# Graph network kernel: norm, query/key/value products and walk table merged into one stage

## What is computed

```python
# layer 0: relational sum, residual and norm
xt  = einsum('ni,rio->rno', x, W0)                 # 8 relations
agg = segment_sum(xt[edge_type, dst], src)         # rows by relation and node
x1  = layernorm(x + relu(agg + bias))
# layer 1: attention over the edges, 8 heads of 32
Q, K, V = x1 @ Wq, x1 @ Wk, x1 @ Wv
score = (K[src] * Q[dst]).sum(head) / sqrt(32) + edge_weight
attn  = softmax of score over the edges of one dst
out   = segment_sum(attn * V[src], dst) @ Wp + bp
# then two layer norms around a GELU network of width 1024,
# the residual x1 and a last layernorm
```

## Time and profile before

| | us |
|---|---|
| median of 3 runs | 5518.05 (5516.32 to 5522.2) |
| the profiled execution, its own time | 5525.3 |
| its span | 5523.6 |
| mid and walk stages in it, from 2551.2 to 2829.0 | 277.8 |

### The profile page before, as it was taken

The page is one execution under the profiler, slowest core; times in us unless marked ns, Lnnn a source line. Parts: engine busy times, 40 slices in busy tenths (PEclk is TensorE's granted clock), DMA queues, the critical chain, the costliest instruction groups (busy, mean ns, idle before and its releaser), DMA issues.

```text
span 5523.6 us, 88413 instructions
## 1 busy us (share of the span) xinstructions
PE 4353.1 (79%) x19107; PEld 2903.1 (53%) x19107; DVE 4710.7 (85%) x15317; ACT 3282.0 (59%) x8872; POOL 3212.9 (58%) x3363
## 2 busy tenths in 40 slices
PE   7998777777777767554848888888888888887997
PEld 3444444344444444443536666666666666665556
DVE  6888999999999998555269999999999999995555
ACT  2888777777777777000236666666666666662222
POOL 2003777777777777772047777777777777760000
PEclk9999999999999999776979999999999999998999
DMA  5433333333333333335347777777777777762000
GB/s 171 132 126 113 105 105 104 105 104 105 105 105 103 101 104 105 105 105 112 118 142 214 215 215 212 212 212 209 212 212 209 212 212 209 211 187 65 6 16 24
DMA packets 349148, 778.95 MB, mean 141 GB/s; under 512 B 76928, under 2 KB 179927, under 8 KB 348629
## 3 DMA queue, kind: packets, MB, share of 16 engines
q0 software_dynamic: 214080, 658.04, 41.8%
q1 hardware_dynamic: 129138, 111.40, 6.4%
q10 hardware_dynamic: 5410, 3.83, 0.2%
HBM read 691.39 MB, written 81.59 MB: 140 GB/s over the span
## 4 chain that ended last, share of the span: by engine, by line
PE 27%; DVE 14%; issue 9%; DVEq 2%; POOL 1%; ACT 1%; DMA 0%; POOLq 0%; ACTq 0%; SPq 0%
PE pb L1412 11%; DVE node_a L1558 4%; PE pb L1396 4%; PE pb L1782 3%; PE pb L1791 3%; DVE big L1516 2%; PE pb L1123 2%; DVE big L1544 1%; DVEq L325 1%; PE pb L1803 1%; PE pb L1129 1%; DVE peak L1583 1%; DVE peak L1585 1%; DVE top L1565 1%; PE pb L1447 1%
## 5 line engine op out<-in xcount | busy, mean ns | idle before, releaser
L1376 POOL DMA_INDIRECT big<-kv_table,walk_s x1664 | 1586.1, 953 | 575.0 <-issue 478.1
L694 POOL DMA_INDIRECT big<-xt_table,big x1616 | 1554.8, 962 | 535.7 <-issue 496.8
L703 ACT ACTIVATE walk_s<-walk_s,big 128x128 bf16<-128x128 bf16 x4704 | 1499.3, 390 | 426.7 <-DVE walk_s L968 402.5
L841 PE MATMUL pb<-big,walk_s 128*128 128x256 f32 x3232 | 1035.1, 417 | 243.8 <-issue 128.5
L1412 PE MATMUL pb<-big,early 128*128 128x264 f32 x3328 | 841.2, 396 | 105.0 <-issue 84.8
L1008 DVE TENSOR_TENSOR node_a<-node_a,pb 128x256 f32 x1616 | 662.9, 410 | 258.1 <-PE pb L841 248.5
L1396 PE MATMUL pb<-node_a,hot_t 128*128 x3328 | 819.7, 389 | 28.8 <-issue 22.8
L841 PEld LDWEIGHTS pb<-big,walk_s 128*128 128x128 f32 x3232 | 621.3, 208 | 385.9 <-DVE walk_s L1032 155.7
L768 PE MATMUL pb<-walk_s 128*128 128x384 bf16 x1568 | 531.5, 339 | 349.6 <-ACT walk_s L703 317.7
L1412 PEld LDWEIGHTS pb<-big,early 128*128 128x128 f32 x3328 | 601.6, 191 | 227.2 <-issue 118.0
L1396 PEld LDWEIGHTS pb<-node_a,hot_t 128*128 128x128 f32 x3328 | 602.9, 191 | 112.9 <-issue 47.2
(11 more groups left out here) (275 smaller groups left out, 5573.3 us busy)
## 6 DMA issues: line engine op xcount, KB each, us to landing
xt_table<-big SPq DMA_DIRECT2D x98, 512.0 KB, 2.9
big<-kv_table,walk_s POOLq DMA_INDIRECT x1664, 3.7
big<-xt_table,big POOLq DMA_INDIRECT x1616
pens<-pen_table SPq DMA_DIRECT2D x832, 12.1 KB
kv_table<-big SPq DMA_DIRECT2D x49, 256.0 KB, 2.0
x_store<-big SPq DMA_DIRECT2D x49, 128.0 KB, 2.0
big<-in_x POOLq DMA_DIRECT2D x48, 128.0 KB, 3.3
big<-in_x SPq DMA_DIRECT2D x6, 1024.0 KB, 11.4
```

The lines of the kernel that those rows point to most:

```text
L694: e.indirect_dma_start(sum_rows[:, q % SUM_ROWS, k, :], None, xt_table, bass.IndirectOffsetOnAxis(ap=idx_all[:, i:i + 1], axis=0))\
L703: ins = e.activation(hot_v[:, t % SORT_HOTS, v, :], hot_q[:, t % SORT_HOTS, :], ACT.Copy, scale=byte[:, t:t + 1])
L841: e.matmul(pb[:, SUM_AT + i % SUM_BANKS, 0:D], sum_hot[:, i % SUM_HOTS, :], sum_rows[:, q % SUM_ROWS, k, :], start=True, stop=True).then_i ...
L1376: e.indirect_dma_start(rows[:, q % ROW_RING, k, 0:2 * D], None, kv_table, bass.IndirectOffsetOnAxis(ap=src_i[:, i:i + 1], axis=0))\
```

## The change

The mid and the walk phase become one. SP, ACT, DVE, TensorE and POOL each run both parts in one order. The buffers of `x` and the walk's records no longer share a region: `x1` becomes a ring of 35 tiles plus one slot for the last tile. The `x` loads are eight (x_loads), Wq, Wk and Wv stand behind the first of them, and loads 5 and 6 (tiles 35 to 42 and 43 to 47) wait until tiles 0 to 7 and 0 to 12 have been stored and transposed. The moments are turned into scales in chunks of eight tiles on DVE alone, by an integer first guess and four Newton steps (`inverse_root`), in place of the one square root on ACT and the reciprocal. Tile w is normalised in step w+10 of DVE's loop and its query copied in step w+13. The walk's DVE instructions are the same and stand in fixed steps of the loop. The query has two PSUM banks in place of four, and banks 6 and 7 serve the walk's matmuls. The ends and carries go through POOL's queue in place of SP's. `dst_i` is `dl_f` now, and `u_row` lies in `hot_t`. The edge phase and everything after it are unchanged.

```diff
+        X_RING = 35
+        x1m = cut((X_RING + 1) * D).rearrange("p (w d) -> p w d", d=D)
+        root_w = cut(2 * 8)
+        def inverse_root(e, c, y, x, t):
+            c(e.tensor_scalar(t.bitcast(I32), x.bitcast(I32), 1, None, ALU.arith_shift_right))
+            c(e.tensor_scalar(y.bitcast(I32), t.bitcast(I32), -1.0, float(0x5f3759df), ALU.mult, ALU.add))
+            for _ in range(4):
+                c(e.tensor_tensor(t, y, y, ALU.mult))
+                c(e.scalar_tensor_tensor(t, t, -0.5, x, ALU.mult, ALU.mult))
+                c(e.scalar_tensor_tensor(y, t, 1.5, y, ALU.add, ALU.mult))
...
+        x_loads = [(0, 8), (8, 16), (16, 24), (24, 32), (32, X_RING), (X_RING, 43), (43, W - 1), (W - 1, W)]
+        NORM_LAG = CHUNK + 2
+        Q_LAG = NORM_LAG + 3
+        REC_AT = 25
...
         def mid_io(e):
+            load(0)
             for n, name in enumerate(("L1_gnn_Wq", "L1_gnn_Wk", "L1_gnn_Wv")):
...
+            load(1)
             e.wait_ge(s_upad, 1)
...
+            for k in (2, 3, 4):
+                load(k)
+            e.wait_ge(s_xpad, 1)
+            load(7)
+            for w in range(W):
+                e.wait_ge(s_norm, w + 1)
+                e.dma_start(x1_store[w * P:(w + 1) * P, :], xs_of(w)).then_inc(s_x1st, 16)
+                e.wait_ge(s_kvc, w + 1)
+                e.dma_start(kv_table[w * P:(w + 1) * P, :], kv_out[:, w % 2, :]).then_inc(s_kvst[w % 2], 16)
+                for k in (5, 6):
+                    if w == x_loads[k][1] - X_RING - 1:
+                        e.wait_ge(s_x1st, 16 * (w + 1))
+                        e.wait_ge(s_nt, w + 1)
+                        load(k)
...
+            def root(ws):
+                lo, n = ws[0], len(ws)
+                c.upto(c.n)
+                c(e.tensor_scalar(root_w[:, 0:n], moments[:, lo:lo + n, 1], EPS, None, ALU.add))
+                inverse_root(e, c, rstd[:, lo:lo + n], root_w[:, 0:n], root_w[:, CHUNK:CHUNK + n])
+                c(e.scalar_tensor_tensor(nmr[:, lo:lo + n], moments[:, lo:lo + n, 0], -1.0, rstd[:, lo:lo + n],
+                                         ALU.mult, ALU.mult))
...
+            for m in range(W + Q_LAG):
+                if m < W:
+                    relu_add(m)
+                if 0 <= m - 1 < W:
+                    count(m - 1)
+                if 0 <= m - 2 < W:
+                    moment(m - 2)
+                    if (m - 2) % CHUNK == CHUNK - 1 or m - 2 == W - 1:
+                        root(chunks[(m - 2) // CHUNK])
+                w = m - NORM_LAG
+                if 0 <= w < W:
+                    if w == 0:
+                        c(e.memset(acc_w[:, :, D:AW], 0.0))
+                    e.tensor_scalar(xs_of(w), xs_of(w), rstd[:, w:w + 1], nmr[:, w:w + 1], ALU.mult, ALU.add)\
+                        .then_inc(s_norm, 1)
+                w = m - Q_LAG
+                if 0 <= w < W:
+                    e.wait_ge(s_qkv, 2 * w + 2)
+                    e.tensor_copy(acc_w[:, w + 1, 0:D], pb[:, 4 + w % 2, 0:D]).then_inc(s_qc, 1)
+                if m == 11:
+                    walk_ends()
+                if m == 15:
+                    walk_spread()
+                if 16 <= m < 16 + WALK_G:
+                    walk_tiles(m - 16)
+                if m == 16 + WALK_G:
+                    walk_index()
+                    select_consts()
+                if 33 <= m < 37:
+                    walk_row(m - 33)
+                if m == 37:
+                    walk_table()
+                if m == 38:
+                    pens_ends()
+                if 39 <= m < 45:
+                    k, odd = divmod(m - 39, 2)
+                    if odd:
+                        pens_out(k)
+                    else:
+                        pens_flag(k)
+                if m == 50:
+                    carries_out()
+                if m == 53:
+                    locals_of()
...
         def mid_tensor(e):
...
+                if w >= 2:
+                    e.wait_ge(s_qc, w - 1)
...
+                if w == 1:
+                    e.wait_ge(s_ucol, 1)
+                    spread(u_col, 0, 4, 6)
+                    spread(u_col, 4, UG, 7).then_inc(s_urow, 1)
+                b = w - 19
+                if 0 <= b < 4:
+                    if b == 0:
+                        e.wait_ge(s_tcol, 1)
+                    if b >= 2:
+                        e.wait_ge(s_wrowd, b - 1)
+                    spread(t_col, 4 * b, min(4 * b + 4, WALK_G), 6 + b % 2).then_inc(s_trow, 1)
+                if 0 <= w - REC_AT < WALK_G:
+                    turn_records(w - REC_AT)
...
         def mid_scalar(e):
-            e.wait_ge(s_stat, 1)
-            e.activation(rstd[:], rstd[:], ACT.Sqrt).then_inc(s_sq, 1)
...
+                if 0 <= w - 1 - REC_AT < WALK_G:
+                    keep_records(w - 1 - REC_AT)
...
-        phase(sync=walk_io, gpsimd=walk_gather, vector=walk_vector, tensor=walk_tensor, scalar=walk_scalar)
+        phase(sync=mid_io, gpsimd=mid_gather, vector=mid_vector, tensor=mid_tensor, scalar=mid_scalar)
```

More of the change, by code:

```diff
@@ L1076, in mid_vector @@
[L1076 to L1131, removed]
@@ L1253, in walk_vector, with locals_of, bias_mask, bias_add @@
+            def locals_of():
+                e.wait_ge(s_recc, 3 * WALK_G)
+                c(e.scalar_tensor_tensor(dl_f, w_row, -float(P), dl_f, ALU.mult, ALU.add))
+            def bias_mask(bound, op):
                 c(e.tensor_scalar(w_tmp, dl_f, bound, LOW, op, ALU.mult))
+            def bias_add():
                 c(e.tensor_tensor(wgt_i, wgt_i, w_tmp, ALU.add))
[L1256 to L1258 removed]
@@ L1266, in walk_vector @@
-            e.sem_inc(s_pens, 1)
-            e.wait_ge(s_endin, 32)
-            first, last = ends_in[0:CHUNKS, :, 0], ends_in[0:CHUNKS, :, 1]
-            con, who = cont[0:CHUNKS, :], whole[0:CHUNKS, :]
-            base, step = (carry_out[0:CHUNKS, k * 2 * SPAN:(k + 1) * 2 * SPAN].rearrange("p (s c) -> p s c", s=2)
-                          for k in range(2))
-            c(e.memset(carry_out, LOW))
-            c(e.memset(step[:, 0, 0:1], 0.0))
-            c(e.memset(cont, 0.0))
-            c(e.tensor_tensor(con[:, 1:SPAN], first[:, 1:SPAN], last[:, 0:CH], ALU.is_equal))
@@ L1283, in walk_vector @@
-            c(e.tensor_scalar(step[:, 1, 1:CH], step[:, 1, 1:CH], 1.0, -LOW, ALU.subtract, ALU.mult))
-            e.sem_inc(s_carry, 1)
-        def walk_tensor(e):
-            def spread(col, n):
-                for g in range(n):
-                    ins = e.matmul(pb[:, g // 4, (g % 4) * P:(g % 4 + 1) * P], col[:, g:g + 1].to_broadcast([P, P]),
+            e.memset(xs_of(W - 1), 0.0).then_inc(s_xpad, 1)
+            e.memset(u_col, 1e6).then_inc(s_upad, 1)
+            for m in range(W + Q_LAG):
[36 more added lines that the diff above has]
+                        pens_out(k)
+                    else:
+                        pens_flag(k)
[3 more added lines that the diff above has]
+                    locals_of()
+                if m == 54:
+                    c(e.tensor_copy(dl_b, dl_f))
+                if m == 55:
+                    bias_mask(0.0, ALU.is_lt)
+                if m == 56:
+                    bias_add()
+                if m == 57:
+                    bias_mask(float(P), ALU.is_ge)
+                if m == 58:
+                    bias_add()
@@ new lines, in mid_tensor, with turn, spread @@
+        def mid_tensor(e):
+            def turn(w):
+                e.wait_ge(s_norm, w + 1)
+                if w >= 2:
+                    e.wait_ge(s_ntc, w - 1)
+                for k in range(KC):
+                    ins = e.transpose(pb[:, w % 2, k * P:(k + 1) * P], xs_of(w)[:, k * P:(k + 1) * P], ident[:])
+                ins.then_inc(s_nt, 1)
+            def spread(col, lo, hi, bank):
+                for g in range(lo, hi):
+                    ins = e.matmul(pb[:, bank, (g - lo) * P:(g - lo + 1) * P], col[:, g:g + 1].to_broadcast([P, P]),
@@ L1310, in walk_scalar @@
                         .then_inc(s_recc, 1)
-        phase(sync=walk_io, gpsimd=walk_gather, vector=walk_vector, tensor=walk_tensor, scalar=walk_scalar)
+            turned(0)
+            for w in range(W):
+                if w + 1 < W:
+                    turned(w + 1)
+                e.wait_ge(s_qkv, 2 * w + 1)
+                if w >= 2:
+                    e.wait_ge(s_kvst[w % 2], 16 * (w // 2))
+                e.activation(kv_out[:, w % 2, :], pb[:, 2 + w % 2, :], ACT.Copy).then_inc(s_kvc, 1)
+                if 0 <= w - 1 - REC_AT < WALK_G:
+                    keep_records(w - 1 - REC_AT)
```

303 lines of the change are left out of this document (172 added, 131 removed).

## The result

| us | before | changed kernel |
|---|---|---|
| median of 4 runs | 5520.12 (5516.32 to 5522.82) | 5419.65 (5417.96 to 5428.29) |
| ratio | | 0.9822, 95% interval 0.9805 to 0.9839 |
| profiled execution, its span | 5525.3, 5523.6 | 5420.85, 5419.1 |
| start of the stage, start of the edge stage | 2551.2, 2829.0 | 2543.0, 2719.4 |
| length between the two | 277.8 | 176.4 |

The time fell by 100.5 us, where the prediction had 100.9; 5419.65 stands against a forecast of 5417. The stage that changed is 101.4 us shorter. The rest of the two profiles also differs, by 8.2 us before the stage and 5.1 us after it in the other direction, though no instruction there was changed; the experiments come back to that.

What follows compares the result with a forecast made beforehand. TensorE was taken to bound the merged stage: first transpose 2569.6 + 149.6 work + 7 stalls = 2726.2, edge stage 1.9 later at 2728.1 instead of 2829.0. That is 100.9 us off the 5518.05 median: 5417 us, range 5405 to 5434.

Steps and rivals of the forecast that it cites:

- front, start of the stage to first transpose: Start of the merged stage: scales after ten tile sums let TensorE's first transpose come at 2569.6, 27.0 us earlier.
- a root: DVE, seven times, once per chunk: a chain of 16 small instructions at 0.21 us, 3.4 us each.
- load 1 late: Second x load, behind Wq, Wk and Wv: lands near 2562.8, wanted at 2563.1; cost 0, at worst 4 us.
- TensorE's work: First transpose to last product: 140.7 us plus 8.9 for added spreads and transposes, 149.6 us.
- waits for norms: TensorE stalls where DVE's norms come late in the merged loop: 7 us in all, bounds 0 and 20.
- records, gathers, stores, query banks late: Queues and waits beside TensorE's work: records have 4.4 us of slack; cost taken as 0, at most 4 us.
- The queue of DVE: DVE's loop: lateness up to 4.2 us is free, each step repays 1.4 us, the rest stalls TensorE, 7 us.
- upper bound of 20 us: Worst TensorE stalls: all walk and root work of steps 16 to 30 and 39 to 45 beyond 1.4 a step.
- Gathers held by DVE: Rival: each of 13 POOL gathers waits for one DVE instruction, 1 to 11 us lost, 5418 to 5428; chance 0.07.
- DVE becomes the bound: Rival: root instructions of 0.47 us or more make roots 7.5 us, 15 to 25 us lost, 5432 to 5442; chance 0.08.
- TensorE loses its clock: Rival: stalls in the merged stage drop the granted clock to 0.50, work becomes 299 us, 5560; chance 0.01.
- The edge stage: Stage after the merged one: may find TensorE's clock up, worth at most 2 to 3 us, taken as 0.

Runs made afterwards that it cites:

- run without walk pieces: Changed kernel with the walk's pieces taken out of the tile loops into a phase of their own behind the products: 5483.68 us, 0.9935 of the kernel before.
- spread run: Changed kernel with the same walk pieces in other steps of DVE's loop, long ones kept apart from roots: 5411.68 us, 0.9805 of the kernel before.
- run with one block moved: Kernel before, with only the block of local targets and bias moved behind the penalties and carries: 5509.15 us, 0.9980 of the kernel before.

## Why the prediction was right

| step of the prediction | predicted | changed kernel |
|---|---|---|
| front, start of the stage to first transpose | 18.4 | 17.9 |
| a root | 3.4 | 3.2 |
| load 1 late | 0 | 0.2 at most |
| TensorE's work | 149.6 | 150.7 busy (149.7 and 149.5 in the other two profiles) |
| waits for norms | 7 | 5.9 |
| records, gathers, stores, query banks late | 0 | 0 |
| last product to edge stage | 1.9 | 1.9 |
| stage | 176.9 | 176.4 |

- **What bounds it.** The reading of the earlier trace rows, that TensorE's middle stretch stays and everything beside it can hide, is what carried the number; no term missed by over 1.1 us. The misses also cancel in part (front 0.5 short, work 1.1 long, waits 1.1 short), and the changed kernel's medians lie between 5415.3 and 5419.7 us, so that the agreement to 0.4 us is luck and that to some 5 us is not.
- **The roots.** Taking 0.21 us from the chain of 128x13 instructions in place of 0.33 from 128x256 was right (0.20).
- **The queue of DVE.** The prediction let backlog up to 4.2 us cost nothing, let each step repay 1.4 us, and placed the losses at the roots of steps 17 and 25 and in steps 39 to 44. The waits stand there: 0.54 against 0.4, 1.32 against 1.9, and at the flags four with 3.7 in all against five with 4.9. The run without walk pieces and the spread run (no wait after the second tile in either) show that it is large pieces too close together, and not the roots or the walk's work as such. The upper bound of 20 us for these waits does not come out of the pieces that it names, which give some 12 to 17 by its own prices; the forecast's own worse bound, 85 us less, would have stood with 17 as well.
- **Gathers held by DVE.** This rival fell: at most 1.08 us. The figure of about 3100 ns that the Trainium skill (page "SBUF — State Buffer", section "SBUF: two separate sides") gives beside a copy did not carry over: none of the 13 gathers stands beside a long copy from SBUF to SBUF, and beside norms, sums and copies out of PSUM of 0.4 us each none took over 1.08 us. Small delays do occur. The longest of the 13 in any run here took 1.42 us, in the run with one block moved: it began at 2770.45, while a 128x831 instruction of DVE (L1242) ran until 2771.04. In the kernel before, a gather beside the same instruction took 0.95, so that the cause stays open. Two rows that the prediction did not use could have settled most of this beforehand: in the kernel before, 1616 gathers of layer 0 (L694, median 0.949 us, longest 1.769) and 1664 of the edge stage (L1376, median 0.949, longest 1.204) already ran in stages where DVE was busy 88% and 97% of the time.
- **DVE becomes the bound.** It didn't, since roots cost 0.20 us an instruction. The run with eight Newton steps built a milder case, with roots of 5.6 us where the rival had 7.5: 14 to 19 us lost where the rival said 15 to 25, 5 to 6 of them by the clock and not by the queue.
- **TensorE loses its clock.** The changed kernel's waits, at most 1.32 us, cost no clock. But the rival was put too coarsely, as a whole stage at half clock or nothing. The runs show an intermediate case: waits of 2 to 4 us, each possibly followed by some microseconds at a lower clock. Here the placing kept clear of it; with roots of 5.6 us, or with chunks of four, it cost 5 to 9 us of busy time that no term of the prediction held. In this respect the forecast had luck.
- **The edge stage.** It did find the clock up (1.00 in the 1.9 us before it; its first four matmuls took 0.40 us against 0.61), but the prediction's 0 can't be told from its 2 to 3 us in rests that scatter from 2693.2 to 2699.7.
- **What it didn't see.** About 10.5 us could be had by the place of one block behind the carries, without merging. The sum was untouched, since all of the walk was hidden, and whether the merged kernel would lose anything with the old order was not run. But the prediction compared stages and not the order inside the walk stage, where DVE stood 7.99 us for ACT's copies.

## What to carry to other kernels

When work of a second engine is laid between the tiles of a full one, reckon it as a queue: how late it may be (slack), how much each step makes good (repayment), and the size of each piece. Averages (forecast as 133 against 146 us here, and 126.7 measured) say that it fits; the placing decides the last 6 us, and it costs nothing to keep two large pieces from falling between the same two norms. Where a piece stands inside its step counts too: one at the end of a step delays the norm of the next. Before merging two stages, look for an order inside each that shortens it alone.

## What the hardware showed that was not expected

- TensorE waits of 2.0 to 3.7 us, with full work around them: nine in the runs with eight Newton steps and with chunks of four. Seven were followed by a granted clock of 0.66 to 0.69 over the next 5 us (four products in 3.15 and 3.46 us instead of 1.88), two, of 2.35 and 3.26 us, by no drop. Waits up to 1.32 us were never followed by one in the changed kernel. What decides between the cases is open.
- A DVE chain of 128x8 instructions, each waiting for the one before, ran at 0.20 us per step. Sixteen took 3.1 to 3.3 us, and 3.5 us once, beside gathers (from 2625.61).
- Splitting a 1 MB load let the first sum start 2.9 us after the stage began, where it was 5.7 us with the load in one piece. The last piece came no sooner: tile 4 could be summed only after 6.9 us, a wait of 1.46 us. With 0.79 MB of weights ahead of load 1 tile 8 waited 2.26 us; with them behind it, it did not wait.
